# Graph and expert layer: the two bias rows of the expert loop gathered per tile and added by DVE instead of multiplied in on PE

## The reference, cut to what matters

```python
gate = xt @ Wg + bg                                   # xt: 1250 x 768
scores, idx = jax.lax.top_k(gate, 2)
h = gelu(einsum('td,edh->eth', xt, W1) + b1[:, None, :])    # 8 experts, hidden 384
y = einsum('eth,ehd->etd', h, W2) + b2[:, None, :]          # back to 768
out = einsum('te,etd->td', comb, y)                         # comb: score at the 2 chosen experts, else 0
x = x + out
```

## Time and profile before

| what | us |
|---|---|
| median of 3 runs (lowest 1107.85, highest 1111.13) | 1110.53 |
| the profiled execution's own time | 1116.81 |
| its span | 1115.1 |
| PE busy | 982.6 (88%) |
| DVE busy | 761.7 (68%) |
| ACT busy | 332.3 (30%) |
| POOL busy | 116.9 (10%) |

### The profile page before, as it was taken

One profiled execution on the slowest core, in us unless ns is written; L12 is line 12 of the kernel. 1 busy time (PEld: TensorE's weight loads), 2 busy tenths in 40 slices (PEclk: granted clock), 3 DMA queues, 4 the chain that ended last, 5 costly groups with the idle time before them and its releaser, 6 DMA issues.

```text
span 1115.1 us, 17266 instructions
## 1 busy us (share of the span) xinstructions
PE 982.6 (88%) x6458; PEld 711.2 (64%) x6460; DVE 761.7 (68%) x1704; ACT 332.3 (30%) x402; POOL 116.9 (10%) x123
## 2 busy tenths in 40 slices
PE   3699999999789989989979988977888669999996
PEld 2677776765454445445769988957774546666663
DVE  6576788877875676986577988689988942233222
ACT  3561122112004332521332432214434522222220
POOL 3010000000001000000000000000604023333322
PEclk9789999999989989999989999968898679999998
DMA  8340121134250927527768100006035635444441
GB/s 233 113 152 30 57 83 61 57 131 182 100 185 30 306 72 243 179 74 260 252 247 376 48 1 1 1 1 253 7 120 203 265 92 103 89 93 100 100 75 20
DMA packets 58266, 139.19 MB, mean 125 GB/s; under 512 B 12308, under 2 KB 31654, under 8 KB 55242
## 3 DMA queue, kind: packets, MB, share of 16 engines
q1 hardware_dynamic: 49290, 112.01, 28.8%
q0 software_dynamic: 6048, 18.31, 8.2%
q10 hardware_dynamic: 2848, 7.77, 1.8%
HBM read 92.10 MB, written 48.90 MB: 126 GB/s over the span
## 4 chain that ended last, share of the span: by engine, by line
PE 68%; DVE 21%; issue 4%; DMA 3%; ACT 2%; SPq 1%; DVEq 0%; POOLq 0%; ACTq 0%
PE PS L1730 39%; PE PS L1979 13%; PE PS L1806 3%; DVE arena L1490 3%; DVE arena L1446 2%; DVE arena L1452 2%; PE PS L2130 2%; PE PS L1817 1%; PE PS L1786 1%; PE PS L1821 1%; DVE arena L1462 1%; DVE arena L1352 1%; DMA arena<-in_L_gnn_W_dram 1%; DVE arena L1202 1%; DMA arena<-as_d 1%
## 5 line engine op out<-in xcount | busy, mean ns | idle before, releaser
L1730 PE MATMUL PS<-arena 128*128 128x384 f16 (+7 forms) x3396 | 576.6, 323 | 6.3 <-DVE arena L1716 1.9
L1730 PEld LDWEIGHTS PS<-arena 128*128 128x128 f16 (+2 forms) x3396 | 322.0, 99 | 218.8 <-issue 16.0
L1979 PE MATMUL PS<-arena 128*128 128x193 f32 (+1 forms) x1200 | 193.5, 325 | 21.9 <-DVE arena L1452 16.5
L1979 PEld LDWEIGHTS PS<-arena 128*128 128x128 f32 x1200 | 189.0, 202 | 26.3 <-DVE arena L1452 16.0
L1016 ACT ACTIVATE arena<-arena,AS 128x1280 f32<-128x1280 f32 x60 | 81.7, 1362 | 135.4 <-DVE arena L1446 135.2
L1720 DVE TENSOR_SCALAR arena<-PS,arena 128x768 f32<-128x768 f32 x27 | 27.5, 1018 | 138.1 <-PE PS L2156 138.1
L1446 DVE SCALAR_TENSOR_TENSOR arena<-arena,AS 128x1280 f32<-128x1280 f32 x60 | 94.2, 1572 | 0.0
L1452 DVE SCALAR_TENSOR_TENSOR arena<-arena 128x1280 f32<-128x1280 f32 x60 | 90.6, 1509 | 4.9 <-PE PS L1979 4.9
L1254 DVE TENSOR_SCALAR arena<-arena 128x240 f16<-128x240 f16 x324 | 88.8, 274 | 0.0
L1253 DVE TENSOR_SCALAR arena<-arena 128x128 f16<-128x128 f16 x324 | 79.8, 246 | 0.1
L1084 ACT ACTIVATE arena<-PS 128x1536 f16<-128x1536 f16 x27 | 39.2, 1450 | 100.4 <-PE PS L2130 100.4
(11 more groups left out here) (274 smaller groups left out, 952.6 us busy)
## 6 DMA issues: line engine op xcount, KB each, us to landing
arena<-in_L_ffn_W_dram SPq DMA_DIRECT2D x48, 384.0 KB, 4.0
fr_d<-arena SPq DMA_DIRECT2D x48, 384.0 KB, 3.4
arena<-fr_d SPq DMA_DIRECT2D x16, 1152.0 KB, 15.0
arena<-in_x_dram SPq DMA_DIRECT2D x18, 384.0 KB, 5.6
arena<-rr_d SPq DMA_DIRECT2D x4, 1280.0 KB, 8.9
g_d<-arena SPq DMA_DIRECT2D x10, 388.0 KB, 2.3
acc_d<-arena SPq DMA_DIRECT2D x10, 384.0 KB, 2.6
xf_d<-arena ACTq DMA_DIRECT2D x10, 384.0 KB, 3.4
```

The costliest lines, as they stand in the source:

```text
L1730: m = T.matmul(out, left[i][x], right[i][y], start=first and i + r == 0, stop=last and 3 * i + r == n - 1)
L1979: m = T.matmul(ps[b][:, r * (C + 1):(r + 1) * (C + 1)], PT[i % deep][:, d * P:(d + 1) * P], feats, start=t == 0 and r == 0, stop=t == NT - ...
```

## The change

The bias products, `sel`, `fb3`, `fbs` and POOL's and SP's work for them go. The two bias tables are copied once, early, into a DRAM table `fb_d` of 8 rows of 1152 f32 numbers (4,608 bytes). In the expert loop POOL gathers for each tile, by its expert numbers `eint`, the same row of `fb_d` into all 128 partitions of one of two buffers `BR[i % 2]`. In POOL's turn j this `bias_gather(j)` stands behind `sums_add(j - 2)`. DVE has two instructions more per tile: `inner(i)` adds the first bias to `up`'s result and writes `Hp` in SBUF, from which ACT takes the gelu; and the second bias is added to `down`'s result before the multiplication by the score, which becomes an instruction of its own on SBUF. In DVE's program `inner(i + 1)` stands between the split of tile i's hidden layer and its result.

```diff
+        BW = HID + D
+        BR = v3(reg(O_X, 2 * BW), 2)
+        Hp = reg(O_X + 2 * BW, HID)
...
+        fb_d = nc.dram_tensor("fb_d", (NE, HID + D), F32, kind="Internal").ap()
...
+            sp.dma_start(fb_d[:, 0:HID], fb1).then_inc(s_row_in, 16)
+            sp.dma_start(fb_d[:, HID:BW], fb2).then_inc(s_row_in, 16)
             sp.wait_ge(s_kv_added, NT)
...
-            sp.wait_ge(s_fbs_blank, 3)
-            for r in (0, 64, 96):
-                sp.dma_start(fbs[r:r + NE, 0:HID], fb1).then_inc(s_fbs_in, 16)
-                sp.dma_start(fbs[r:r + NE, HID:HID + D], fb2).then_inc(s_fbs_in, 16)
...
-            sp.wait_ge(s_bias_high, 5)
             for u in freed:
                 experts(u)
...
-            g.memset(fbs, 0.0).then_inc(s_fbs_blank, 1)
...
-            for r in range(4):
-                fconst(g.iota(pidi[32 * r:32 * r + 32, :], [[1, 1]], base=0, channel_multiplier=1))
-            fconst(g.tensor_copy(pidx, pidi))
...
-            pool.wait_ge(s_fbs_in, 96)
-            g.tensor_copy(fb3, fbs).then_inc(s_bias_high, 1)
-            for n, r in enumerate((64, 96)):
-                pool.wait_ge(s_bias_high, 1 + 2 * n)
-                g.tensor_tensor(fbs[r:FBR, :], fbs[r:FBR, :], fb3[r:FBR, :], ALU.subtract).then_inc(s_bias_high, 1)
-                pool.wait_ge(s_bias_high, 2 + 2 * n)
-                g.tensor_copy(fb3[r:FBR, :], fbs[r:FBR, :]).then_inc(s_bias_high, 1)
-            pool.wait_ge(s_bias_high, 5)
...
+            def bias_gather(i):
+                g.indirect_dma_start(out=BR[:, i % 2, :], out_offset=None, in_=fb_d,
+                                     in_offset=bass.IndirectOffsetOnAxis(ap=eint[:, i:i + 1].bitcast(U32), axis=0)).then_inc(brows_in[i % 2], 16)
...
             for i in range(3):
                 rows_gather(i)
+            pool.wait_ge(s_slots_ready, 1)
+            pool.wait_ge(s_row_in, 16 * 7)
+            pool.wait_ge(s_map_psum, 2)
+            for i in range(2):
+                bias_gather(i)
             pool.wait_ge(s_x2_out, 16 * NT)
             for i in range(NTL + 2):
                 if i + 3 < NTL:
...
                 if i >= 2:
                     sums_add(i - 2)
+                    if i < NTL:
+                        bias_gather(i)
...
+            def gelu(i):
+                act.wait_ge(s_hp_ready, i + 1)
+                if i:
+                    act.wait_ge(s_ht_psum, i)
+                a.activation(Hb, Hp, ACT.Gelu).then_inc(s_h_ready, 1)
...
-            V.tensor_copy(eint, eid)
-            V.tensor_scalar(sel[:, 0:NTL], eid[0:FBR, :], pidx[0:FBR, :], UP, ALU.is_equal, ALU.mult).then_inc(s_slots_ready, 1)
+            V.tensor_copy(eint, eid).then_inc(s_slots_ready, 1)
...
+            def inner(i):
+                dve.wait_ge(brows_in[i % 2], 16 * (i // 2 + 1))
+                dve.wait_ge(s_h_psum, i + 1)
+                if i:
+                    dve.wait_ge(s_h_ready, i)
+                V.scalar_tensor_tensor(Hp, ps[2 + i % 2][:, 0:HID], 1 / UP, BR[:, i % 2, 0:HID], ALU.mult, ALU.add).then_inc(s_hp_ready, 1)
+
+            Y = PS[:, 5 * 512:7 * 512].rearrange("p (a n) -> p a n", a=2)[:, :, 0:HALF]
+            inner(0)
             for i in range(NTL):
...
                 V.tensor_tensor(ht[:, 1], ps[4][:, 0:HID], ht[:, 0], ALU.subtract).then_inc(s_ht_ready, 1)
+                if i + 1 < NTL:
+                    inner(i + 1)
+                yb = Yb[:, i % 2, :]
                 dve.wait_ge(s_y_psum, i + 1)
                 if i >= 2:
                     dve.wait_ge(sums_out[i % 2], 16 * (i // 2))
-                V.tensor_scalar(Yb[:, i % 2, :].rearrange("p (a n) -> p a n", a=2), PS[:, 5 * 512:7 * 512].rearrange("p (a n) -> p a n", a=2)[:, :, 0:HALF], score[:, 1, i:i + 1], None, ALU.mult).then_inc(s_y_ready, 1)
+                link(V.scalar_tensor_tensor(yb.rearrange("p (a n) -> p a n", a=2), Y, 1 / UP, BR[:, i % 2, HID:BW].rearrange("p (a n) -> p a n", a=2), ALU.mult, ALU.add))
+                V.tensor_scalar(yb, yb, score[:, 1, i:i + 1], None, ALU.mult).then_inc(s_y_ready, 1)
...
             def up(i, e):
                 pe.wait_ge(s_xrt_ready, i + 1)
                 if i >= 2:
-                    pe.wait_ge(s_h_ready, i - 1)
+                    pe.wait_ge(s_hp_ready, i - 1)
...
-                T.matmul(ps[2 + i % 2][:, 0:HID], sel[:, i:i + 1].to_broadcast([FBR, P]), fb3[:, 0:HID], start=False, stop=True).then_inc(s_h_psum, 1)
...
-                    m = T.matmul(ps[5 + c][:, 0:HALF], sel[:, i:i + 1].to_broadcast([FBR, P]), fb3[:, HID + c * HALF:HID + (c + 1) * HALF], start=False, stop=True)
...
-            pe.wait_ge(s_bias_high, 5)
```

More of the change, by code:

```diff
@@ L282, in gps_layer @@
         seqh = small(P // 2).bitcast(F16)
-        pidx = small(1)
-        pidi = small(1).bitcast(I32)
         upper = small(P // 2).bitcast(F16)
         onesh = small(1).bitcast(F16)
[L287 to L290, removed]
         xf_d = nc.dram_tensor("xf_d", (NP + P, D), F32, kind="Internal").ap()
         acc_d = nc.dram_tensor("acc_d", (NP, D), F32, kind="Internal").ap()
+        fb_d = nc.dram_tensor("fb_d", (NE, HID + D), F32, kind="Internal").ap()
         bias_d = nc.dram_tensor("bias_d", (D,), F32, kind="Internal").ap()
@@ L473, in gps_layer @@
         s_x2_out = sem("x2_out")
-        s_fbs_blank = sem("fbs_blank")
-        s_fbs_in = sem("fbs_in")
-        s_bias_high = sem("bias_high")
+        s_o2t_blank = sem("o2t_blank")
+        s_brow0_in = sem("brow0_in")
+        s_brow1_in = sem("brow1_in")
+        s_hp_ready = sem("hp_ready")
         s_nt_psum = sem("nt_psum")
@@ L513, in gps_layer @@
         sums_out = (s_sum0_out, s_sum1_out)
+        brows_in = (s_brow0_in, s_brow1_in)
         assert NT % 2 == 0
@@ L520, in gps_layer @@
         CONST = 10
-        FCONST = 19
+        FCONST = 14
         GROUPS = ((0, HALFT), (HALFT, NT - 2), (NT - 2, NT))
@@ L805, in _ @@
                 r = KS + 1 - h
[L806 to L811, removed]
+                g.tensor_scalar(WUB[0:r, h, :], WUB[0:r, h, :], UP, None, ALU.mult).then_inc(s_o2t_blank, 1)
+                pool.wait_ge(s_o2t_blank, 3 + 3 * h)
+                g.tensor_copy(wuh[0:r, h, :], WUB[0:r, h, :]).then_inc(s_o2t_blank, 1)
+                pool.wait_ge(s_o2t_blank, 4 + 3 * h)
+                g.tensor_tensor(wul[h][0:r, :], WUB[0:r, h, :], wuh[0:r, h, :], ALU.subtract).then_inc(s_o2t_blank, 1)
+                pool.wait_ge(s_o2t_blank, 5 + 3 * h)
             pool.wait_ge(s_o2t_psum, 4 + len(OUT2))
@@ L1085, in _ @@
                 if i:
[L1086 to L1092, removed]
+                    gelu(i - 1)
+            gelu(NTL - 1)
         @block.vector
@@ L1707, in _ @@
             link(V.tensor_tensor(score[:, 0, :], score[:, 0, :], mapped(2), ALU.add))
-            link(V.tensor_scalar(score[:, 1, :], score[:, 0, :], 128 / UP, None, ALU.mult))
+            link(V.tensor_scalar(score[:, 1, :], score[:, 0, :], 128.0, None, ALU.mult))
+            def inner(i):
[6 more added lines that the diff above has]
+            inner(0)
             for i in range(NTL):
@@ L2046, in fin @@
                 if t == 0:
-                    pe.wait_ge(s_fbs_blank, 9)
+                    pe.wait_ge(s_o2t_blank, 8)
                 if t >= 2:
@@ L2135, in up @@
                 if i >= 2:
-                    pe.wait_ge(s_h_ready, i - 1)
+                    pe.wait_ge(s_hp_ready, i - 1)
                 product(ps[2 + i % 2][:, 0:HID], [(XRTP[:, i % 2, 0, k, :], XRTP[:, i % 2, 1, k, :]) for k in range(KC)],
-                        [[FR[:, 0, bass.ds(e, 1), r, k * HID:(k + 1) * HID] for r in (HI, LO)] for k in range(KC)], last=False)
-                T.matmul(ps[2 + i % 2][:, 0:HID], sel[:, i:i + 1].to_broadcast([FBR, P]), fb3[:, 0:HID], start=False, stop=True).then_inc(s_h_psum, 1)
+                        [[FR[:, 0, bass.ds(e, 1), r, k * HID:(k + 1) * HID] for r in (HI, LO)] for k in range(KC)]).then_inc(s_h_psum, 1)
             def turn(i):
@@ L2153, in down @@
                 for c in range(2):
-                    product(ps[5 + c][:, 0:HALF], [(HT[:, i % 2, 0, k, :], HT[:, i % 2, 1, k, :]) for k in range(HC)],
-                            [[FR[:, 1, bass.ds(e, 1), r, k * D + c * HALF:k * D + (c + 1) * HALF] for r in (HI, LO)] for k in range(HC)], last=False)
-                    m = T.matmul(ps[5 + c][:, 0:HALF], sel[:, i:i + 1].to_broadcast([FBR, P]), fb3[:, HID + c * HALF:HID + (c + 1) * HALF], start=False, stop=True)
+                    m = product(ps[5 + c][:, 0:HALF], [(HT[:, i % 2, 0, k, :], HT[:, i % 2, 1, k, :]) for k in range(HC)],
+                            [[FR[:, 1, bass.ds(e, 1), r, k * D + c * HALF:k * D + (c + 1) * HALF] for r in (HI, LO)] for k in range(HC)])
                 m.then_inc(s_y_psum, 1)
```

6 lines of the change are left out of this document (3 added, 3 removed).

## The result

The changed kernel takes 1216.01 us (median of 4 runs, 1213.51 to 1217.47), the kernel before 1110.83 in the same series; the ratio is 1.094 with a 95% interval of 1.090 to 1.098. It is 105 us slower. Forecast were 1197, between 1156 and 1242.

A forecast was written before the change was run, and what follows sets the result against it. PE bound the expert loop at 7.33 us a tile; the new ring takes 10.86, so 274.2 us for 26 steps against 188.9 (+85.3), plus 1.6 at the head: +86.9 on 1110.5 gives 1197.4 us, range 1156 to 1242.

The forecast's parts named there:

- The ring: Expert loop, result to result: sum's issue, gather's issue, its landing, three DVE instructions; 10.86 us a tile.
- signs that were named beforehand: Loop: PE about two thirds busy, longest waits at `inner`, result right behind it, steps about 10.9 us, landings 5.5 to 6.
- wake and issue: Loop, POOL: result's end to sum's issue 0.82 us, from there to the gather's issue 1.89.
- The landing of the bias gather: Loop, gather from `fb_d` behind the sum: 5.8 us after issue, bounds 3.8 and 7.65.
- allowance for light tiles: Loop: three tiles with few real pairs, gather landing at 3.8 to 4.2 instead of 5.1; together 3.3 us less.
- DVE's three instructions: Loop, DVE after the landing: `inner` 0.56 us, result from PSUM 1.02, multiplication on SBUF 0.66.
- The head: Loop's start: first bias gather lands at 911.4 us, `up(0)` is done at 910.6; +1.6 us in all.
- What I booked at zero: Ahead of the loop: POOL's removed bias work, slot 14's earlier transfer and the two copies into `fb_d` change nothing.
- The tail: Behind the last result: as before, no change.
- Rival 1: Loop: gather doesn't queue behind the sum, lands in 3.8 us, 8.86 a tile, 1151 us in total; chance 0.12.
- Rival 2: Loop: PE's clock falls to 0.50 throughout, PE needs 13.7 us a tile, 1275 us in total; chance 0.08.
- Rival 3: Loop: bias lands in time, within 2.3 us for no loss, PE stays the bound, 1098 us in total; chance 0.03.

The follow-up runs named there:

- the version with the result first: The changed kernel, two buffers, with DVE's inner(i+1) moved behind the result of tile i: 1187.1 us, 10.25 us a step.

## Why the prediction was right, and where it was not

**The ring: right.** The page's row on who waits, the chain and three cuts at different places of it (a buffer, DVE's order, POOL's order) all behave as the ring says: 6.8, 10.25 and 7.05 us a tile against 11.4. Of the signs that were named beforehand, PE's share (70%), who waits for whom and the result right behind `inner` came; the landing at 5.5 to 6 did not.

**Its size: 11.6 instead of 10.86 a tile.** By terms of the sum: wake and issue 0.8 + 1.9, as taken. The landing of the bias gather had a median of 6.9 instead of 5.8, with bytes right, the shared DRAM row left out (0.5 to 0.8), the rest open. Its mean over the 25 steps is 6.74, where the forecast with its allowance for light tiles comes to 5.67: 27 us in all. DVE's three instructions took 2.1 instead of 2.3 (`inner` hands over after 0.48, the result took 0.96, the score product 0.62), which gives 6 of them back. The forecast's support for the place behind the sum was also weaker than it says: in the trace of before the row gather landed 1.3 to 1.5 us after the sum in 13 of 21 turns, not 18, and 0.9 to 3.0 us after it in the others. From the first to the last sum this gives 297.4 us instead of the 274.2 forecast, so +108.6 and not +85.3. 1.6 us of that is the last step, 7.6 instead of 6.0, in which PE's products ran partly at 1.2 GHz.

**The head: +0.9 instead of +1.6.** First gather to first sum 22.3 us against 21.4.

**What I booked at zero: not zero.** "So I book nothing" for POOL's preparation was wrong by 5 us in the other direction. I had looked for who waits for POOL, and on the chain nobody does; the cost was in DVE instructions that last longer beside it, which stand in the timeline of before as a 48-column instruction of 2.30 us, and in PE's clock behind them. The Trainium skill says it plainly ("GPSIMD Engine Reference", section "1. Specifications"): the SBUF interfaces of GpSimd are shared with VectorE, and there is contention with VectorE instructions that have two SBUF inputs or run in a two-port mode. The trace agrees for L1641 (2.30 us) and L1632 (1.65), which have two inputs; for the TENSOR_SCALAR that stood at 2.27, which has one, no row shows the mode.

**The tail: +2.2 instead of nothing.** From the last sum's start to the end of the span it is 8.5 us in every version with the bias gather and 6.2 or 6.3 in the kernel before and its version without the subtractions. What is in it the trace doesn't name; left open.

Together 108.6 + 0.9 - 5 + 2.2 = 106.7, where the medians differ by 105.2. The forecast's 86.9 was 18 short. That it was no further off is in part luck: the landing alone was 27 short, and 6 us too much for DVE's instructions and 5 for the work ahead of the loop, booked at nothing, went the other way.

**Rival 1** (the gather doesn't queue behind the sum) was wrong for this kernel, and the kernel with the bias gather ahead of the sum shows what it would have needed: there the landing is 4.5. The Trainium skill's estimate for the transfer alone, 3.4 us ("DMA: Bandwidth & Descriptors", section "Anatomy of one DMA — SWDGE (gpsimd) path"), stays under every landing of 590 KB that was seen, 4.1 us at least.

**Rival 2** (the clock) was half right. The clock did fall, to a mean of 0.86, as the Trainium skill ("TensorE: Matmul & The Clock Gate", section "Why this matters for your kernels") warns for idle gaps. In the changed kernel PE isn't in the ring and has time to spare, which absorbs it; that part was argued from the waits and not tried alone. In the version with the result first PE is in the ring, and there it cost 20 us in the loop.

**Rival 3** (the bias comes in time) is what three buffers make of it: 1100.9 us, where I had priced 1098. Its condition, a landing within 2.3 us, was not met there either (6.6); the third buffer gives the same landing one tile more of time.

## What to carry to other kernels

When work moves from the engine that is the bound to idle ones, follow the waits once around instead of adding up idle time: a transfer that may only be issued when a buffer comes free, and whose reader stands ahead of the instruction that frees the next buffer, closes a ring of one iteration, and every latency in it is paid each time. One more buffer, or issuing the load before the store, is worth more than the whole change (115 and 114 us here, against 12 by which the loop of the three-buffer version is shorter than that of the kernel before). And look for small instructions with a long duration beside a busy neighbour engine before booking the neighbour's work at nothing.

## What the runs showed of the hardware that I had not expected

- A gather in which all 128 partitions read one DRAM row of 4,608 bytes landed 0.8 us later than one in which each read its own (6.9 against 6.1, medians of 27 in one execution each; the steps differ by 0.5).
- An indirect gather issued behind an accumulating transfer landed 2.4 us later than the same gather issued ahead of it (6.9 against 4.5).
- DVE instructions of 0.1 to 0.7 us took up to 2.3 beside POOL's two-input subtractions; the small ones ended within 0.1 us of them, and one ended with a one-input cast of POOL's in the same way. Instructions with an operand in PSUM were not lengthened.
- Twelve useless products per tile made a kernel faster, 266.6 to 246.1 us in the loop; the granted clock there was 1.00 instead of 0.91.
